# Layer 0 of a four-layer graph kernel: PE transposes replaced by DMA transposes, the row scaling moved to VectorE, and two row tiles' products grouped

## What is computed

```
adj: 2048 x 2048, a 0/1 mask whose rows are divided by their sums
w = einsum('nd,dkio->nkio', embedding, weight)      # D = 16, K = 3
b = embedding @ bias
As = [I, adj, 2 * adj @ adj - I]
x_g = einsum('knm,bmc->bnkc', stack(As), x)
x = layernorm(x + einsum('bnki,nkio->bno', x_g, w) + b)
```

## Time and profile before

| | us |
|---|---|
| median of 3 runs (1029.78 to 1030.65) | 1029.88 |
| the profiled execution, its own time | 1030.52 |
| its span | 1028.7 |

### The profile page before, as it was taken

One profiled execution on the slowest core, in us unless ns is written; L12 is line 12 of the kernel. 1 busy time (PEld: TensorE's weight loads), 2 busy tenths in 40 slices (PEclk: granted clock), 3 DMA queues, 4 the chain that ended last, 5 costly groups with the idle time before them and its releaser, 6 DMA issues.

```text
span 1028.7 us, 18675 instructions
## 1 busy us (share of the span) xinstructions
PE 1009.2 (98%) x6864; PEld 485.6 (47%) x6864; DVE 677.5 (66%) x1680; ACT 456.6 (44%) x1109; POOL 559.7 (54%) x653
## 2 busy tenths in 40 slices
PE   9999999999999999999999999999999999999995
PEld 3445444444444444433445556555555545455552
DVE  4886565666567786586567767886663646657556
ACT  4632333453355545543643454432556655232632
POOL 0005487876668698879878465474534233323311
PEclk9999999999999999999999999999999999999998
DMA  9930000000000000000010111000032231000022
GB/s 369 406 139 1 1 1 2 1 2 1 1 1 2 1 1 2 1 2 1 1 42 1 41 42 42 2 1 1 4 120 107 99 124 42 4 2 21 21 62 62
DMA packets 14659, 45.67 MB, mean 44 GB/s; under 512 B 960, under 2 KB 9280, under 8 KB 10080
## 3 DMA queue, kind: packets, MB, share of 16 engines
q1 hardware_dynamic: 14560, 44.39, 11.7%
HBM read 40.19 MB, written 4.19 MB: 43 GB/s over the span
## 4 chain that ended last, share of the span: by engine, by line
PE 80%; DVE 10%; POOL 3%; ACT 3%; DMA 2%; issue 2%; SPq 0%; POOLq 0%; ACTq 0%; DVEq 0%
PE PS L966 28%; PE PS L929 21%; PE PS L796 20%; DMA BW<-at_in 2%; PE PS L781 2%; PE PS L783 2%; PE PS L782 2%; DVE BW L1232 1%; DVE T L1235 1%; DVE X L1235 1%; DVE X L1548 1%; POOL X L1753 1%; ACT WZ L1079 1%; PE PS L790 1%; PE PS L789 1%
## 5 line engine op out<-in xcount | busy, mean ns | idle before, releaser
L796 PE MATMUL PS<-BW,S 128*128 128x512 fp8e4 x1280 | 290.9, 379 | 1.2 <-DVE R L1235 0.7
L1079 ACT ACTIVATE T<-PS,SM 128x128 f32<-128x128 f32 x384 | 112.9, 366 | 202.3 <-DVE X L1235 127.6
L929 PE MATMUL PS<-WZ,R 64*128 64x512 f16 x1536 | 197.8, 377 | 0.0
L796 PEld LDWEIGHTS PS<-BW,S 128*128 128x128 f16 x1280 | 120.1, 98 | 148.5 <-issue 15.3
L966 PE MATMUL PS<-BW,S 128*128 128x512 fp8e4 x768 | 173.1, 379 | 0.1
L1753 POOL TENSOR_TENSOR T<-T 128x128 f32<-128x128 f32 (+1 forms) x192 | 125.1, 651 | 74.0 <-ACT T L1079 56.7
L1235 DVE SCALAR_TENSOR_TENSOR X<-PS,SM,X 128x128 f32<-128x128 f32 x320 | 109.6, 343 | 76.0 <-PE PS L929 75.9
L929 PEld LDWEIGHTS PS<-WZ,R 64*128 64x128 f16 x1536 | 69.5, 94 | 102.6 <-issue 26.3
L966 PEld LDWEIGHTS PS<-BW,S 128*128 128x128 f16 x768 | 73.8, 98 | 83.3 <-issue 0.5
L966 PE MATMUL PS<-BW,T 128*128 128x512 fp8e4 x480 | 109.3, 379 | 0.0
L1753 POOL TENSOR_TENSOR S<-R,S 128x512 f16<-128x512 f32 (+1 forms) x46 | 52.7, 1152 | 102.8 <-ACT S L1079 102.8
(11 more groups left out here) (213 smaller groups left out, 1515.9 us busy)
## 6 DMA issues: line engine op xcount, KB each, us to landing
WZ<-a_in SPq DMA_DIRECT2D x16, 1024.0 KB, 4.8
BW<-at_in SPq DMA_DIRECT2D x8, 1024.0 KB, 18.7
R<-at_in SPq DMA_DIRECT2D x7, 1024.0 KB, 12.7
out<-X SPq DMA_DIRECT2D x16, 256.0 KB, 2.3
X<-x_in SPq DMA_DIRECT2D x3, 1024.0 KB, 20.8
T<-w_in SPq DMA_DIRECT2D x1, 1536.0 KB, 15.8
R<-at_in SPq DMA_DIRECT2D x2, 512.0 KB, 4.5
SM<-sm_in SPq DMA_DIRECT2D x1, 520.5 KB, 18.9
```

Source lines behind the costliest of these rows:

```text
L796: m = e.matmul(o, stile(h, t, c), Bm[:, t, block(j)], start=(t == 0 and h == 0), stop=(last and t == NT - 1 and h == 1))
L929: m = e.matmul(bank(b0 + q), halves[kd][zh][r, :], WZ[r, wh, kd, block(g)], start=(i == 0), stop=(i == 8))
L1079: return e.activation(o, i, f, **kw)
```

## The change

- **`dx` and `t1` are gone** from PE, DVE, ACT and POOL. SP does both by DMA transposes: `turned_x(u)` is 8 transposes of 128 x 128 blocks of `S` into `DX`, which now has `DXS` = 5 slots of one unit each; `turned_ax(u)` is 2 transposes of 128 x 512 from `T` into `S`.
- **The row scale** comes as a row: the diagonal of adj, copied to all partitions (1 MB, `dr_in`), is loaded into `row_r`, clamped and divided by 64 by DVE at row tile 10. New steps `F1` and `F2` multiply a whole bank in place by it on DVE, before ACT's high half and DVE's low half. The embedding is no longer multiplied by `rmax`.
- `row_r` takes the place of one landing buffer: `RING` is 6.
- **Grouping.** `middle_order` puts two quarters (four in units 1, 2, 5, 6) ahead of two row tiles' `Z` instead of one (two) ahead of each. `F` stays right behind its product; `E1`/`E2` is put between the two groups of the first `Z` behind it.

```diff
-RING = 7
+RING = 6
+DXS = 5
 HEAD = ([("R", jt) for jt in range(9)]
-        + [("E1", 0), ("R", 9), ("R", 10), ("E1", 1), ("R", 11), ("R", 12), ("E1", 2), ("R", 13), ("E1", 3), ("R", 14), ("R", 15)]
+        + [("F1", 0), ("R", 9), ("R", 10), ("E1", 0), ("F1", 1), ("R", 11), ("R", 12), ("E1", 1), ("F1", 2), ("R", 13), ("E1", 2),
+           ("F1", 3), ("R", 14), ("R", 15), ("E1", 3)]
         + [("dg",)]
-        + pieces("P1", 0) + [("E1", 4), ("E1", 5), ("wm",), ("E1", 6), ("E1", 7), ("E1", 8)]
-        + pieces("P1", 1) + [("nb",), ("wn",), ("E1", 9), ("dx", 0), ("t1", 0), ("dx", 1), ("t1", 1), ("dx", 2)]
+        + pieces("P1", 0) + [("F1", 4), ("F1", 5), ("E1", 4), ("E1", 5), ("wm",), ("F1", 6), ("F1", 7), ("E1", 6), ("E1", 7), ("F1", 8), ("E1", 8)]
+        + pieces("P1", 1) + [("nb",), ("wn",), ("F1", 9), ("E1", 9)]
         + [("xs", 0)]
-        + pieces("P1", 2) + [("t1", 2), ("dx", 3), ("t1", 3), ("xs", 1), ("E1", 10), ("bounds",)]
-        + pieces("P1", 3)[0:3] + pieces("P2", 0) + [("E2", 0), ("P1", 3, 3), ("E1", 11)])
+        + pieces("P1", 2) + [("xs", 1), ("F1", 10), ("bounds",), ("E1", 10)]
+        + pieces("P1", 3)[0:3] + pieces("P2", 0) + [("F2", 0), ("E2", 0), ("P1", 3, 3), ("F1", 11), ("E1", 11)])
...
-        each = len([x for x in beside if x[0][0] == "P"]) // 4
-        for t in range(4):
+        each = len([x for x in beside if x[0][0] == "P"]) // 2
+        for t in (0, 2):
...
+                x = beside.pop(0)
+                (later if x[0] in ("E1", "E2") else order).append(x)
+            for i in (t, t + 1):
+                order += [("Z", u, i, 0), *later, ("Z", u, i, 1), ("add", u, i)]
+                order += after.pop(4 * u + i, [])
+                later = []
...
+            def turned_x(u):
+
+                c, j = divmod(u, 4)
+                if u < DXS:
+                    e.wait_ge(s_bm, (26, 28)[u // 4])
+                    e.wait_ge(s_xlo, NT)
+                else:
+                    e.wait_ge(s_zp, 8 * (u - DXS + 1))
+                for k in range(4):
+                    for h in range(2):
+                        e.dma_start_transpose(DX[:, u % DXS, h, 128 * k:128 * k + 128].unsqueeze(1),
+                                              stile(h, 4 * j + k, c)).then_inc(s_dx[u % DXS], 16)
+
+            def turned_ax(u):
+
+                c, j = divmod(u, 4)
+                e.wait_ge(s_p1, 10 + 2 * c)
+                e.wait_ge(s_u1, first_index(c, j) + 1)
+                e.wait_ge(s_dx[u % DXS], 128 * (u // DXS + 1))
+                for h in range(2):
+                    e.dma_start_transpose(spart(h, c, j), T[:, c, h, block(j)]).then_inc(s_t1[j], 16)
...
+            for u in range(DXS):
+                turned_x(u)
+            for u in range(4):
+                turned_ax(u)
+            for u in range(4, 16):
+                if u >= DXS:
+                    turned_x(u)
+                turned_ax(u)
...
-            e.wait_ge(s_t1, 4 * c + q + 1)
+            e.wait_ge(s_t1[q], 32 * (c + 1))
...
+        def dve_f1(e, n):
+            c, j = divmod(n, 2) if n < 8 else UNITS[n - 8]
+            b = bank(n if n < 8 else unit_bank["P1", n - 8])
+            e.wait_ge(s_p1, n + 1)
+            e.tensor_tensor(b, b, row_r[:, block(j)], ALU.mult).then_inc(s_f1, 1)
+
+        def dve_f2(e, u):
+            e.wait_ge(s_p2, u + 1)
+            stt(e, bank(0), bank(0), 2.0, row_r[:, block(u % 4)], ALU.mult, ALU.mult).then_inc(s_f2, 1)
...
+                elif jt == 10:
+                    e.wait_ge(s_dr, 16)
+                    vc(ts(e, row_r, row_r, 1.0 / 512, 1.0, ALU.max, ALU.min))
+                    ts(e, row_r, row_r, 1.0 / EDGE, None, ALU.mult).then_inc(s_row_r, 1)
```

More of the change, by code:

```diff
@@ L614, in take_banks @@
                         continue
-                    if kind in ("dx", "t1"):
-                        done = (s_dx if kind == "dx" else s_t1e, step[1] + 1)
-                    elif kind == "mean":
+                    if kind == "mean":
                         done = (s_msum, step[1] + 1)
@@ L906, in tensor_steps @@
                 elif kind == "Z":
-                    u, t = step[1:]
+                    u, t, g = step[1:]
                     c, j = divmod(u, 4)
[L909 to L931, removed]
+                    if g == 0:
+                        e.wait_ge(s_dx[u % DXS], 128 * (u // DXS + 1))
+                        e.wait_ge(s_u2, u + 1)
+                        e.wait_ge(s_wlo, 1)
@@ new lines, in tensor_steps @@
+                    k0, k1 = slice(128 * (4 * j + t), 128 * (4 * j + t) + 128), slice(128 * t, 128 * t + 128)
+                    halves = ([DX[:, u % DXS, h, k1] for h in range(2)], [T[:, c, h, k0] for h in range(2)],
+                              [U2[:, u % 3, h, k1] for h in range(2)])
+                    n = 2 * (4 * u + t) + g
+                    b0 = z_bank(n)
+                    if n < 3:
+                        for b in (b0, b0 + 1):
+                            e.wait_ge(*z_first[b])
+                    else:
+                        e.wait_ge(s_za, 3 * (n - 2))
@@ L932, in tensor_steps @@
+                    for i in range(9):
+                        kd, part = divmod(i, 3)
+                        zh, wh = ((0, 0), (0, 1), (1, 0))[part]
+                        for q in range(2):
+                            r = slice(64 * q, 64 * q + 64)
+                            m = e.matmul(bank(b0 + q), halves[kd][zh][r, :], WZ[r, wh, kd, block(g)],
+                                         start=(i == 0), stop=(i == 8))
+                    m.then_inc(s_zp, 1)
                 elif kind == "mean":
@@ L1052, in act_e1 @@
                 e.wait_ge(s_xc, 4 * (n - 10))
[L1053 removed]
+            e.activation(T[:, c, 0, block(j)], bank(b), ACT.Copy).then_inc(s_u1h, 1)
         def act_e2(e, u):
[L1056 removed]
+            e.wait_ge(s_f2, u + 1)
             if u >= 3:
                 e.wait_ge(s_zp, 8 * (u - 2))
[L1059 to L1066, removed]
[L1067 to L1075 removed]
+            elif u == 0:
+                e.wait_ge(s_bm, 2 * NT)
+            e.activation(U2[:, u % 3, 0, :], bank(0), ACT.Copy).then_inc(s_u2h, 1)
         def scalar_steps(e, steps):
@@ L1097, in scalar_steps @@
                 elif kind == "Z":
-                    u, t = step[1:]
+                    u, t, g = step[1:]
                     c, j = divmod(u, 4)
                     n4, it = 4 * u + t, 4 * j + t
-                    if n4:
+                    if n4 and g == 0:
                         e.wait_ge(s_ab, n4)
[L1103 to L1108, removed]
-                               scale=emb[:, it, 8 * g + d:8 * g + d + 1]).then_inc(s_za, 1)
+                    e.wait_ge(s_acc[0], 5 * n4 + (3, 5)[g])
+                    e.wait_ge(s_acc[1], 5 * n4 + (2, 5)[g])
+                    ps = zpair(2 * n4 + g)
+                    for d in range(DV, 8):
+                        fn(grid(AT[:, 3 * g + d - DV, :]), ps[:, :, d, :], ACT.Copy,
+                           scale=emb[:, it, 8 * g + d:8 * g + d + 1]).then_inc(s_za, 1)
                 elif kind == "sq":
```

162 lines of the change are left out of this document (51 added, 111 removed).

## The result

| | before | after |
|---|---|---|
| median of 4 runs each, us | 1030.27 (1029.78 to 1030.85) | 1055.26 (1053.68 to 1056.87) |
| ratio after to before, 95% interval | | 1.0242 [1.0225, 1.026] |
| span of the profiled execution, us | 1028.7 | 1053.7 |
| PE busy, us | 1009.2 | 994.4 |
| first and last start of layer 0's weights, us | 107.6, 521.6 | 137.0, 545.6 |

The changed kernel is slower by 2.4%, 25 us. The forecast, 1012.2, was wrong, and so was its sign; 1055 also lies above the range given, 1008 to 1040. Rival R2 is what happened.

A forecast was written before the change was run, and what follows sets the result against it. PE was taken to bound the kernel, busy 1009 of 1028.7 us. Terms -14.4 - 2.3 (waits gone) - 6.7 + 4.1 + 0.6 + 1 = -17.7 us gave 1012.2 us from the median 1029.88; range 1008 to 1040.

The forecast's parts named there:

- R2: Rival: SP's queue of transposes becomes the bound; 1053 us at b = 0.85, 1078 at the packet bound; chance 0.24.
- The transposes: SP's transposing DMAs, in the head and at chunk borders, meet their deadlines: 0 us.
- b: SP's time per transposed block of 128 x 128: 0.42 us taken, 1.06 at the packet bound.
- a: SP's time per transpose of 128 x 512: about 0.8 us taken, 4.2 at the packet bound.
- budgets: SP's time before PE needs the data: 40b + 8a under 35.4 us in the head, 8b + 2a under 8.6 at borders.
- Removed from PE: 32 dx and t1 steps of 0.45 us leave PE, eight in the head, 24 in the middle: 14.4 us gained.
- Grouping: In the middle, 32 fewer round trips between full-height and half-height matmuls on PE, 0.21 us each: 6.7 us gained.
- The head: Added DVE work (row_r) and later mask tiles and E1 make PE wait before the first P1 unit: 4.1 us lost.
- `F2`: DVE's scaling in the chain behind the first P2, 2.3 us against 1.73 of covering quarter: 0.6 us lost.
- R1: Rival: transposes somewhat late, between b = 0.49 and 0.66, eating up the gain: 1018 to 1030 us; chance 0.15.
- Four groups in a row: Middle: some weight groups come late as DVE and ACT free the banks; 1 us lost, between 0 and 16.
- R3: Rival: four weight groups in a row starve PE, 0.3 to 0.5 us in 32 places: 1022 to 1028 us; chance 0.08.

The follow-up runs named there:

- batch_nogroup: batch with the old order, one quarter ahead of each row tile's weights instead of two ahead of two: 1024.3 us, ratio 0.9937 to the kernel before.
- batch: The changed kernel with S laid out so one instruction turns 128 x 512, 64 transposes instead of 160: 1019.72 us, ratio 0.9895 to the kernel before.
- batch_mean: batch with the steps mean and row_a put one row tile later: 1014.72 us, ratio 0.9845 to the kernel before.

## Why the prediction was wrong, point by point

**The transposes: the step that failed.** It priced a transpose by the issue of a plain DMA: b at 0.42, because an issue row has the same 128 partitions, and a at 0.8, and so the whole term at 0 us. The term was 32.2 us of waits. Measured: b = 1.30 in the head, 1.26 to 1.44 at the borders, and a = 1.26 to 1.31. b lies above my upper bound of 1.06, which I had made from packets, and a far under its bound of 4.2: neither bound had the right form, since I let the cost grow with rows and bytes, and it goes by instruction. A row for one kind of DMA does not bound another kind. The text named the right signs, "SP's issues end to end" and 0.5 us as the point where it would fall.

Its budgets, on the other hand, held. With b = a = 1.27 they give 48 x 1.27 - 35.4 = 25.6 us late in the head and 3 x (10 x 1.27 - 8.6) = 12.3 at the borders. Measured: 23.09 + 0.69 + 0.69 = 24.5 and 2.52 + 1.90 + 3.34 = 7.8. The head is right to 1 us. At a border I had charged two full landings; the timeline shows SP going on 227.86 - 226.67 = 1.2 us after its last block has been issued, since a landing of 2.4 counts from the start of the issue, of which 1.27 is already in the term. That the three border waits differ is the issues again, SP's timeline of the changed kernel at the second and third border:

```profile
324.25 10.06 SPq L737 DMA_TRANSPOSE R<-S  x8
...
422.76 11.52 SPq L737 DMA_TRANSPOSE R<-S  x8
```

The eight blocks ahead of each border took 10.73, 10.06 and 11.52 us, and PE waited 2.52, 1.90 and 3.34. Why single blocks take longer there (up to 2.5 us) is not shown.

The Trainium skill, "Advanced Engine Details and Errata", section "X-Bar Transpose (TRN2)", says that transposing DMAs are as fast as regular ones. The trace agrees for the landing, 2.4 us against 2.3, and not for the issue, 1.26 to 1.31 against 0.37 to 0.42.

**R2** was given 0.24. I read it at a = 4b, where it decides from b = 0.66; with a = b it decides from 1.0, and with the measured 1.27 it gives 1012.2 + 37.9 = 1050, against 1055.3. The rest is in the points on `mean` and on the clock.

**Removed from PE, 14.4 us: about right.** With few transposes and no grouping (batch_nogroup), where the two steps alone are gone, PE's busy time fell by 1009.2 - 996.7 = 12.5 us. Grouping takes off more: together it is 18.1 in batch and 14.8 in the changed kernel, which has more stretches at the lower clock; "about 20" had been said. The waits of L834 are gone.

**Grouping, 6.7 us: the size of the piece right, its worth not a number by itself.** Two tiles with two quarters take 148.40 - 136.97 = 11.43 us in the changed kernel:

```profile
148.40 0.82 PE L930 MATMUL PS<-WZ,R 64*128 64x512 f16 x6
```

against 2 x 5.82 = 11.64, so 0.21 a round trip as read. But with the few transposes it brought 4.6, in the changed kernel -3.9, and in the kernel before it lost 7 to 11, because it moves PE ahead of DVE, POOL and SP, and shortens their time. With `mean` moved as well it brought 1024.30 - 1014.72 = 9.6, more than 6.7, as it also takes away eight of the nine waits for DVE. (batch_nogroup has no wait at `mean`; moving it there was not tried.)

**The head, 4.1 us: right.** Forecast 66.4 for the first quarter of `P1` 0 and 72.4 for its fourth, measured 66.37 and 72.53. PE began mask tile 13 at 53.96, as forecast; its wait there shows as 0.95, behind one of 0.71 for ACT at 49.39. `row_r` took DVE 2.4 us and cost PE nearly all of it: undoing it brought 2.7. **`F2`**: 0.6 forecast, 0.42 measured (133.41); the three pieces that the forecast adds up, 0.68, 0.60 and 0.7, make 1.98 and not 2.3, which would have given 0.25. (R1's lower edge has a slip too: at b = 0.49 nothing is late yet, so it begins at 1012 and not at 1018.) SP started at 65.14, forecast 65.1.

**Four groups in a row, 1 us: right as asked, but too narrow a question.** PE waits for ACT inside the weights for 0.9 us once in batch and never in the changed kernel; R3 is out. What I did not ask is who else is late when PE moves ahead of the others in the written order: POOL's `sum` for `mean`. It stood at 1.05 us in the kernel before, a wait of PE that I left among the small ones, and is 5.3 in the changed kernel, 4.5 in batch. Moving the step brought 5.0.

**Adding it up.** The miss is 1055.3 - 1012.2 = 43.1 us. Of it 35.5 are the number of transposes (after less batch), 5.0 are `mean` (batch less batch_mean), and 2.6 are left over. Without the first two the forecast was 2.5 us off: batch_mean is 1014.72. Part of that closeness is luck, two misses that offset each other. Without grouping the sum gives 12.0 us of gain, and batch_nogroup gained 1030.57 - 1024.30 = 6.3; for the grouping the sum gives 6.7 - 1 = 5.7, and with `mean` moved it brought 9.6.

## What to carry to other kernels

When work is moved to a queue, count its instructions first and price them by a row of that very kind; if there is none, give the unknown price both forms, by instruction and by byte, and build the data so that few large ones do the same (here 160 to 64 by one layout, 35.5 us). What waits at the queue's end is paid by all that stands ahead of it. A gain on the engine that bounds is also a shorter deadline for every other: look through its small waits of before, and move those steps back with it.

## What the runs showed of the hardware

- A transposing DMA from SBUF to SBUF held SP for 1.2 to 1.3 us (1.30 on average over the 40 blocks of the changed kernel, 1.31 over ten of 128 x 512 in batch, single ones up to 2.5), for 128 x 128 and for 128 x 512 of f16 alike, about three times a plain one of this kernel, and landed in 2.4 to 2.5 us (medians). Over the 23 us of PE's wait the DMA engines were 17% busy.
- PE's granted clock can fall while it stands still, and the matmuls that follow pay again. In the changed kernel it was 0.54 over the 23 us wait and 0.51 for the 3 us after it: half speed, 1.2 instead of 2.4 GHz, and 16 matmuls took 5.01 us instead of 3.63. Some of the short waits do it too. Windows of batch, one with most of the wait that ended at 473.14, and the two behind it:

```profile
470.00:473.00 3.00, 0.51 (x6) 0.01 (x2) 1.38 (x5) 0.00 (x0) 2.77 (x5) 1.00 0.00 0
473.00:478.00 5.00, 4.86 (x16) 2.10 (x17) 0.49 (x2) 3.99 (x9) 4.61 (x7) 0.66 0.00 0
478.00:483.00 5.00, 5.00 (x45) 2.09 (x45) 2.87 (x8) 2.45 (x6) 4.16 (x7) 1.00 0.01 3
```

  The 16 matmuls behind this wait of 2.63 us took 5.30 instead of 3.62 us, 1.7 more; the waits of 2.63 and 2.65 for POOL in the changed kernel cost the same again. But the wait's length alone does not decide it: in the changed kernel PE waited 3.34 us for a DMA until 439.34, and the clock stayed full:

```profile
439.40:443.00 3.60, 3.60 (x26) 1.52 (x28) 0.70 (x1) 0.60 (x1) 3.28 (x6) 1.00 0.00 0
```

  Behind the 1.86 us at 378.38 it stayed full too. Why it fell in one place and not in the other stays open. Nor did the clock of one profiled execution show up whole in the medians: with the 4.5 us of waits for `mean` only 5.0 went, not 6.
